# Post-LN linear attention and gated FFN on one NeuronCore: attention's output too is turned in 32x32 blocks and through DRAM, and the order of a pass is rewritten

## What is computed

```python
qkv = relu(einsum('bnc,oc->bno', x, qkv_weight)); q, k, v = (qkv[:, :, j] for j in range(3))   # after a reshape
v_pad = concatenate([v, ones], axis=-1)
vk = einsum('bnhe,bnhd->bhed', v_pad, k)
vk_q = einsum('bhed,bnhd->bnhe', vk, q)
att = vk_q[..., :8] / (vk_q[..., 8:] + 1e-15)
x1 = layernorm(x + einsum('bnc,oc->bno', att, proj_weight) + proj_bias)
h = silu(x1 @ (w_gate/127).T) * (x1 @ (w_up/127).T)
out = layernorm(x1 + h @ (w_down/127).T)
```

## Time and profile before

| | us |
|---|---|
| median of 3 runs | 555.39 (554.58 to 556.39) |
| the profiled execution's own time | 555.23 |
| its span in the profile | 553.3 |
| TensorE busy | 525.3 (95%) |
| VectorE busy | 409.2 (74%) |
| ScalarE busy | 223.5 (40%) |
| GpSimd busy | 89.4 (16%) |

### The profile page before, as it was taken

How to read it: one execution, slowest core, us unless ns; L and a number is a source line. 1 busy time by engine, 2 the same in 40 slices (tenths; PEclk the granted TensorE clock), 3 DMA queues, 4 the chain that set the end, 5 groups by cost and what they waited for, 6 DMA issues and landing times.

```text
span 553.3 us, 9205 instructions
## 1 busy us (share of the span) xinstructions
PE 525.3 (95%) x3419; PEld 455.5 (82%) x3419; DVE 409.2 (74%) x913; ACT 223.5 (40%) x376; POOL 89.4 (16%) x94
## 2 busy tenths in 40 slices
...
GB/s 302 155 0 78 39 99 93 115 114 63 127 38 114 114 76 152 38 102 88 114 114 71 119 39 113 114 76 152 38 106 84 114 114 71 119 3 113 39 40 39
DMA packets 27918, 51.07 MB, mean 92 GB/s; under 512 B 2304, under 2 KB 17408, under 8 KB 27904
## 3 DMA queue, kind: packets, MB, share of 16 engines
...
## 4 chain that ended last, share of the span: by engine, by line
PE 78%; DVE 11%; DMA 3%; issue 3%; ACT 2%; POOL 1%; SPq 1%; DVEq 0%; POOLq 0%; ACTq 0%
PE abcd_ps L632 27%; PE gate_ps L632 24%; PE up_ps L632 22%; PE abcd_ps L659 3%; DVE x1T_lo L377 2%; PE abcd_ps L678 2%; DVE st L440 2%; DVE r L469 2%; DMA wg_raw<-w_gate 1%; DVE h L384 1%; DMA wd_raw<-x_way 1%; DMA xT_raw<-x_chan 1%; PE abcd_ps L670 1%; ACT h_hi L269 1%; DVE h_lo L377 1%
## 5 line engine op out<-in xcount | busy, mean ns | idle before, releaser
L632 PE MATMUL gate_ps<-x1T_hi,wg_hi 128*128 128x512 f32 x192 | 78.1, 407 | 15.3 <-DVE x1T_lo L377 15.3
L274 ACT ACTIVATE silu<-gate_ps 128x512 f32<-128x512 f32 x96 | 56.9, 593 | 77.7 <-PE gate_ps L632 77.7
L226 POOL TENSOR_TENSOR ve<-mv,ln_eps 128x4 f32<-128x4 f32 (+2 forms) x36 | 12.5, 346 | 444.7 <-DVE mv L446 444.7
L269 ACT ACTIVATE h_hi<-h 128x512 fp32r<-128x512 f32 x96 | 60.2, 633 | 48.0 <-DVE h L384 48.0
L632 PE MATMUL up_ps<-x1T_lo,wu_hi 128*128 128x512 f32 x192 | 74.9, 390 | 0.0
L632 PE MATMUL gate_ps<-x1T_lo,wg_hi 128*128 128x512 f32 x192 | 74.9, 390 | 0.0
L632 PE MATMUL up_ps<-x1T_hi,wu_hi 128*128 128x512 f32 x192 | 74.9, 390 | 0.0
L384 DVE SCALAR_TENSOR_TENSOR h<-up_ps,silu 128x512 f32<-128x512 f32 x96 | 64.2, 681 | 3.8 <-ACT silu L274 3.7
L377 DVE TENSOR_TENSOR h_lo<-h,h_hi 128x512 fp32r<-128x512 f32 x96 | 62.8, 680 | 1.7
L632 PEld LDWEIGHTS gate_ps<-x1T_hi,wg_hi 128*128 128x128 f32 x192 | 36.0, 188 | 25.2 <-DVE x1T_lo L377 18.7
L266 ACT ACTIVATE kv<-abcd_ps 128x512 f32<-128x512 f32 x60 | 35.9, 600 | 46.2 <-PE abcd_ps L632 46.2
...
## 6 DMA issues: line engine op xcount, KB each, us to landing
x_raw<-x_tok SPq DMA_DIRECT2D x16, 512.0 KB, 3.8
xT_raw<-x_chan SPq DMA_DIRECT2D x15, 512.0 KB, 3.3
out<-out_sb SPq DMA_DIRECT2D x15, 512.0 KB, 2.9
x_way<-wu_raw SPq DMA_DIRECT2D x56, 128.0 KB, 2.6
wd_raw<-x_way SPq DMA_DIRECT2D x14, 512.0 KB, 3.2
x<-r SPq DMA_DIRECT2D x14, 512.0 KB, 2.9
...
```

The costliest lines, as they stand in the source:

```text
L226: nc.gpsimd.tensor_tensor(ve[:, tiles], mv[:, tiles, 1], ln_eps[:, tiles], ALU.add).then_inc(ve_ok, 1)
L269: nc.scalar.activation(dst, src, ACT.Copy).then_inc(ok, 1)
L274: nc.scalar.activation(silu[:, j % 2, :], gate_ps[j % 2][:], ACT.Silu, scale=WSCALE).then_inc(silu_ok[j], 1)
L632: last = mm(dst, lhsT, rhs, start=start and n == 0, stop=stop and n == len(pairs) - 1)
```

## The change

att of batches 2 to 15 goes the way of x1: `att_blocks` transposes it in 32x32 blocks into att_sq (memory of the raw gate weights), DMAs write it to att_way and read it back into attT_raw (memory of the raw kv weights), and `attT_hi_spread` and `attT_lo_spread` take hi and lo. Only batches 0 and 1 use `attT_of`. For x1 and att the block transposes, writes, reads and hi parts go by halves of the channels, each half with its own semaphores. The transposes now read channels s*4 + j with s running fastest; a write is one run of 2 KB per partition, and the read takes pieces of 512 B.

In the attention half TensorE does kv first, then q, vk (into bank CC), one tile of down, num, and three tiles of down. The second wait of `gate_up(b, 1)`, for the second add of r2, stands ahead of its up part. VectorE adds the epsilon (`variance`), GpSimd only takes the power. VectorE makes x1, its blocks, then h_lo of blocks 4 and 5, the output of batch i-2, vk, xT_lo two batches ahead, x1T_lo, att and its blocks of batch i+1, and only then both adds of r2 and their statistics. x and xT are loaded, and xT_hi made, a batch earlier.

The diff, cut to its core (and its margin to fit):

```diff
-x1_sq = in_place_of(wu_raw).rearrange("p (c n) -> p c n", c=NCB)
+x1_sq = in_place_of(wu_raw).rearrange("p (k n) -> p k n", k=KC)
 x1T_raw = in_place_of(wd_raw).rearrange("p (k n) -> p k n", k=KC)
-x1_way = nc.dram_tensor("x1_way", (P, KC, NG, P), FP32, kind="Internal").ap()
+att_sq = in_place_of(wg_raw).rearrange("p (k n) -> p k n", k=KC)
+attT_raw = wkv_raw[:].rearrange("p a b -> p (a b)").rearrange("p (k n) -> p k n", k=KC)
+x1_way, att_way = (nc.dram_tensor(n, (KC, P, TB), FP32, kind="Internal").ap() for n in ("x1_way", "att_way"))
...
-    def spread_x1(b):
-        sp.wait_ge(x1_sq_ok, b)
-        for g in range(NG):
-            sp.dma_start(x1_way[:, :, g, :].rearrange("(j c) k n -> c k j n", j=NG),
-                         x1_sq[g * SQ:(g + 1) * SQ].rearrange("c (k j) n -> c k j n", k=KC)).then_inc(x1_away, 16)
-        sp.wait_ge(x1_away, 16 * NG * b)
-        sp.dma_start(x1T_raw, x1_way.rearrange("p k g n -> p k (g n)")).then_inc(x1T_in, 16)
+    def write_blocks(n, sq, sq_ok, way, away):
+        for k in range(KC):
+            sp.wait_ge(sq_ok[k], n)
+            sp.dma_start(way[k], sq[:, k, :]).then_inc(away[k], 16)
+    def read_turned(n, way, away, T_raw, T_in):
+        for k in range(KC):
+            sp.wait_ge(away[k], 16 * n)
+            sp.dma_start(T_raw[:, k, :], way[k].rearrange("(g s) (j n) -> s j g n", g=NG, j=NG)
+                         .rearrange("s j g n -> (s j) g n")).then_inc(T_in[k], 16)
     def turn(i):
         any_i = not isinstance(i, int)
+        if any_i or i + 2 < NB:
+            load_xT(i + 2)
+        if any_i or 0 < i < NB - 1:
+            write_blocks(i, x1_sq, x1_sq_ok, x1_way, x1_away)
+            read_turned(i, x1_way, x1_away, x1T_raw, x1T_in)
         if any_i or i >= 2:
             sp.wait_ge(out_ok, i - 1)
             sp.dma_start(out[i - 2], out_sb[:].rearrange("p t c -> p (t c)")).then_inc(stored, 16)
-        if any_i or i + 1 < NB:
-            sp.wait_ge(xb_ok, i + 1)
-            sp.dma_start(x_raw[:], x[i + 1]).then_inc(x_in, 16)
         if any_i or i + 2 < NB:
-            load_xT(i + 2)
+            sp.wait_ge(xb_ok, i + 2)
+            sp.dma_start(x_raw[:], x[i + 2]).then_inc(x_in, 16)
         if any_i or 0 < i < NB - 1:
-            spread_x1(i)
+            write_blocks(i, att_sq, att_sq_ok, att_way, att_away)
             sp.wait_ge(r2_ok[1], i)
             sp.dma_start(x1[:], r1[:]).then_inc(x1_copied, 16)
+            read_turned(i, att_way, att_away, attT_raw, attT_in)
     sp.dma_start(xT_raw[:, 0, :], xT[0][:, 0, :]).then_inc(xT_half_in[0], 16)
...
-    def rstd(b, mv, mv_ok, ve, ve_ok, rs, rs_ok, tiles=slice(0, NT)):
-        pool.wait_ge(mv_ok, b + 1)
-        nc.gpsimd.tensor_tensor(ve[:, tiles], mv[:, tiles, 1], ln_eps[:, tiles], ALU.add).then_inc(ve_ok, 1)
+    def rstd(b, ve, ve_ok, rs, rs_ok, tiles=slice(0, NT)):
         pool.wait_ge(ve_ok, b + 1)
         nc.gpsimd.tensor_tensor(rs[:, tiles], ve[:, tiles], minus_half[:, tiles], ALU.pow).then_inc(rs_ok, 1)
...
-    with pool.Fori(1, NB - 1) as i:
-        pool.wait_ge(den_ok, i + 1)
+    xb_of(1)
+    rstd_1(1)
+    with pool.Fori(2, NB - 1) as i:
+        pool.wait_ge(h_lo_ok[NH - 1], i - 1)
         xb_of(i)
+        rstd_2(i - 2)
         rstd_1(i)
-        rstd_2(i - 1)
-    pool.wait_ge(den_ok, NB)
+    pool.wait_ge(h_lo_ok[NH - 1], NB - 2)
     xb_of(NB - 1)
+    rstd_2(NB - 3)
...
+    def attT_hi_spread(b):
+        act.wait_ge(proj_mm[1], b)
+        for k in range(KC):
+            act.wait_ge(attT_in[k], 16 * (b - 1))
+            rounded(by_token(attT_hi, k), spread(attT_raw, k), attT_hi_ok[k])
     def x1T_hi_spread(b):
         act.wait_ge(up_mm[NH - 1], b)
-        act.wait_ge(x1T_in, 16 * b)
-        for k in range(KC):
-            rounded(by_token(x1T_hi, k), x1T_spread(k), x1T_hi_ok[k])
+        for k in range(KC):
+            act.wait_ge(x1T_in[k], 16 * b)
+            rounded(by_token(x1T_hi, k), spread(x1T_raw, k), x1T_hi_ok[k])
...
+    def step(i):
+        for j in range(NH - 2):
+            silu_of(i - 1, j)
+            if j < NH - 3:
+                h_hi_of(i - 1, j)
+        if isinstance(i, int) and i == 1:
+            attT_hi_of(i)
+        else:
+            attT_hi_spread(i)
+        h_hi_of(i - 1, NH - 3)
+        silu_of(i - 1, 4)
+        silu_of(i - 1, 5)
         h_hi_of(i - 1, 4, 5)
-        if qkv:
+        if not isinstance(i, int) or i < NB - 1:
+            for t in range(NT):
+                kv_relu(t, i + 1, abcd[:, t, :])
             q_relu(i + 1)
-            for t, bank in enumerate((CC, D, A, B)):
-                kv_relu(t, i + 1, bank)
+            if not isinstance(i, int) or i + 2 < NB:
+                xT_hi_of(i + 2)
             x1T_hi_spread(i)
...
+    def variance(b, mv, mv_ok, ve, ve_ok, tiles=slice(0, NT)):
+        dve.wait_ge(mv_ok, b + 1)
+        nc.vector.tensor_scalar(ve[:, tiles], mv[:, tiles, 1], LN_EPS, None, ALU.add).then_inc(ve_ok, 1)
...
+    def blocks_turned(sq, r, oks):
+        for k in range(KC):
+            nc.vector.transpose(sq[:, k, :].rearrange("p (j t s) -> p t j s", j=NG, t=NT),
+                                r[:, :, k * P:(k + 1) * P].rearrange("p t (s j) -> p t j s", j=NG)).then_inc(oks[k], 1)
     def x1_blocks(b):
         dve.wait_ge(x1_ok, b + 1)
-        nc.vector.transpose(x1_sq.rearrange("p c (t s) -> p t c s", t=NT),
-                            r1[:].rearrange("p t (c s) -> p t c s", s=SQ)).then_inc(x1_sq_ok, 1)
+        blocks_turned(x1_sq, r1, x1_sq_ok)
+    def att_blocks(b):
+        dve.wait_ge(att_ok, b + 1)
+        blocks_turned(att_sq, att, att_sq_ok)
+    def T_lo_spread(b, T_raw, T_hi, T_hi_ok, T_lo, T_lo_ok):
+        for k in range(KC):
+            dve.wait_ge(T_hi_ok[k], b + 1)
+            minus_hi(by_token(T_lo, k), spread(T_raw, k), by_token(T_hi, k)).then_inc(T_lo_ok[k], 1)
+    def attT_lo_spread(b):
...
     def ffn_half(i):
-        att_of(i)
+        late = not isinstance(i, int) or i > 1
+        if late:
+            dve.wait_ge(st2_ok, i - 1)
         h_of(i - 1, 0)
-        if not isinstance(i, int) or i > 1:
-            out_of(i - 2)
+        if late:
+            aggregated(st2, mv2, mv2_ok)
+            variance(i - 2, mv2, mv2_ok, ve2, ve2_ok)
         h_of(i - 1, 1)
-        h_lo_of(i - 1, 0, 1)
+        h_lo_of(i - 1, 0)
         h_of(i - 1, 2)
-        if not isinstance(i, int) or i < NB - 1:
-            xT_lo_of(i + 1)
+        h_lo_of(i - 1, 1)
         h_of(i - 1, 3)
-        attT_lo_of(i)
-        h_lo_of(i - 1, 2, 3)
-        h_of(i - 1, 4, 5)
+        if late:
+            attT_lo_spread(i)
+        else:
+            attT_lo_of(i)
+        h_lo_of(i - 1, 2)
+        h_of(i - 1, 4)
+        h_lo_of(i - 1, 3)
+        h_of(i - 1, 5)
...
-        h_lo_of(i - 1, 4, 5)
+        variance(i, mv1, mv1_ok, ve1, ve1_ok)
         x1_of(i, r1)
         x1_blocks(i)
-        r2_add(i - 1, 0, x1)
-        dve.wait_ge(r2_ok[0], i)
+        h_lo_of(i - 1, 4, 5)
+        if not isinstance(i, int) or i > 1:
+            out_of(i - 2)
+        vk_of(i + 1)
+        if not isinstance(i, int) or i + 2 < NB:
+            xT_lo_of(i + 2)
+        x1T_lo_spread(i)
+        att_of(i + 1)
+        att_blocks(i + 1)
+        for n in range(2):
+            r2_add(i - 1, n, x1)
+        dve.wait_ge(r2_ok[1], i)
         stats(st2, r2, 0)
-        vk_of(i + 1)
-        r2_add(i - 1, 1, x1)
-        dve.wait_ge(r2_ok[1], i)
         stats(st2, r2, 1, st2_ok)
...
     i = NB - 1
     ffn_half(i)
     h_lo_of(i - 1, 4, 5)
+    out_of(i - 2)
     r1_of(i, pairs=True)
...
-            if j == 1 and (not isinstance(b, int) or b > 0):
+            late = j == 1 and (not isinstance(b, int) or b > 0)
+            if late:
                 pe.wait_ge(r2_ok[0], b)
-                pe.wait_ge(r2_ok[1], b)
...
+            if late:
+                pe.wait_ge(r2_ok[1], b)
             add_up(up, up_hi[:-1], stop=False)
...
         pe.wait_ge(xT_lo_ok, i + 2)
+        for t in range(NT):
+            if t >= 2:
+                pe.wait_ge(r1_ok[t - 2], i + 1)
+            kv_of(t, i + 1, abcd[:, t, :])
+        for k in range(KC):
+            pe.wait_ge(kv_ok[k], i + 2)
         q_of(i + 1)
-        for t, bank in enumerate((CC, D, A, B)):
-            if t < 2:
-                pe.wait_ge(r1_ok[t], i + 1)
-            else:
-                pe.wait_ge(q_ok[t - 2], i + 2)
-            kv_of(t, i + 1, bank)
-        down_of(i - 1, (0, 1))
         vk_of(i + 1)
-        down_of(i - 1, (2, 3))
+        down_of(i - 1, (0,))
         num_of(i + 1)
+        down_of(i - 1, range(1, NT))
```

More of the change, by code:

```diff
@@ L24 @@
 SQ = 32
-NG, NCB = P // SQ, C // SQ
+NG = P // SQ
 BANK = 512
@@ L132, in build @@
         x1T_mm, x1T_hi_ok, x1T_lo_ok = signals("x1T_mm", KC), signals("x1T_hi_ok", KC), signals("x1T_lo_ok", KC)
-        x1_copied, x1_sq_ok, x1_away, x1T_in = signal("x1_copied"), signal("x1_sq_ok"), signal("x1_away"), signal("x1T_in")
+        x1_copied = signal("x1_copied")
```

(21 more changed lines are left out.)

59 lines of the change are left out of this document (26 added, 33 removed).

## The result

The changed kernel takes 557.98 us (median of 20 runs, 554.93 to 560.54), the kernel before 554.86 us (20 runs, 553.02 to 556.62). The ratio is 1.0044, with a 95% interval of 1.0027 to 1.0062: **slower by 0.4%**, where 533.4 us was forecast and a range of 528.5 to 548. The profiled execution took 555.09 us for a span of 552.9, 0.4 less than the span before.

What follows compares the result with a forecast made beforehand. TensorE (31.4 us a pass) and a ring through VectorE (31.3) were taken as level bounds; 31.5 a pass saves 1.67 in 14 passes, 23.4, less 1.5 at the ends: 533.4 us from 555.3, range 528.5 to 548.

Steps and rivals of the forecast that it cites:

- TensorE's sum: TensorE's work in one loop pass without att's transposes and the x1T_lo stall: 31.38 us, 1.79 less per pass.
- The ring: Loop's chain of work and waits from r1's first add to the next pass's: 31.3 us, level with TensorE's 31.4.
- the price of the strided transposes: VectorE's block transposes reading every fourth channel, 16 bytes apart: no extra cost taken, bounds nothing and a doubling.
- the walk: Step-by-step sum of the ring's times from r1's first add: 31.7 us, less 0.4 for overlaps, 31.3.
- moves under the output's normalisation: GpSimd's x+bias (2.4 us) shifts beside VectorE's output step in the loop, said to cost nothing.
- the rule that the prediction itself quoted: Skill's SBUF rule: each access crossing to a new 16-byte line pays a penalty of unstated size; every new transpose element does.
- The trip through DRAM: Write and read back of one 256 KB half: 5.8 us, bounds 4.3 and 7.7, VectorE's near 5 us beside it.
- SP's worst place: att's reads queued behind the copy of r1: done at 27.0 at worst, wanted at 27.5 to 28, so covered.
- Numerators ahead of three tiles of down: TensorE's order, one down tile covering vk: hidden if TensorE is slower, costs up to 0.6 where the ring is.
- The ends: First and last batches outside the steady loop: 1.5 us lost in all, 1.1 of it in the last batch.
- the ring is longer: Rival, 19%: slow transfer, slowed silu chain or late att reads make passes of 32.0 to 32.9, 540 to 552 us.
- strided transposes: Rival, 12%: transposes at double price, 2.4 us a pass on the ring, 33.7 a pass, 564 us; slower from 1.8.

Runs made afterwards that it cites:

- e3: Changed kernel with the edits of e1 and e2 together; output not the reference's: 529.45 us, ratio 0.955 to the kernel before.
- e2: Changed kernel with block transposes reading neighbouring channels, not every fourth; output not the reference's: 538.25 us, ratio 0.971 to the kernel before.
- e1: Changed kernel with GpSimd's x+bias started behind den of the same half, not behind h_lo: 547.07 us, ratio 0.988 to the kernel before.
- e5: Changed kernel with VectorE taking vk ahead of the output's normalisation: 550.13 us, ratio 0.994 to the kernel before.
- e4: Changed kernel with ScalarE taking the silu of block j+1 ahead of h_hi of block j: 548.99 us, ratio 0.991 to the kernel before.
- e6: Changed kernel with the 8 transposes of att put back on TensorE, results unused: 561.22 us, ratio 1.0126 to the kernel before.

## Why the prediction was wrong

**TensorE's sum was right but for 0.45 us.** 31.38 a pass was forecast; 30.93 is what e3 has, without a wait. That is 6 us in 14 passes, and one reason why e3 ends below the forecast. The difference is in restarts and modelled ends: three tiles of down and one 5.93 for 6.05, numerators 1.87 for 2.05, gate, up and proj 13.78 for 14.01.

**The ring was the right bound, its length was not.** I walked it to 31.3 and put it level with TensorE; it is 33.14. Two terms failed, both taken at nothing: the price of the strided transposes, worth 1.4 us a pass (33.13 to 31.74 in e2; from e1 to e3 32.33 to 30.93), and that of GpSimd's x+bias, worth 0.8 (33.13 to 32.33 in e1; from e2 to e3 31.74 to 30.93). Since TensorE sets the pass in e3, each is worth at least that. With only one of them the time stays inside the stated range of 528.5 to 548: 547.07 us in e1, just inside, and 538.25 in e2. Against the walk's points, counted from the first add of r1:

| point | walk | measured |
|---|---|---|
| x1 done | 6.4 | 6.0 |
| its transposes done | 7.75 | 8.1 |
| x1T_lo done | 14.8 | 15.8 |
| att done | 17.5 | 18.5 |
| its transposes, r2, statistics done | 21.8 | 23.3 |
| first h done | 22.5 | 24.0 |
| fourth h done | 28.1 | 29.6 |
| next r1 | 31.3 | 33.1 |

- *One failed step, the smaller in the time*, is the one sentence on GpSimd: its x+bias "moves under the output's normalisation", at no cost. It is 2.14 us, on one instruction that stands still. I took 1.4 to 1.7 for an output of 3.52. The trace of before shows it, and I did not ask. The three rows below are its timeline of GpSimd, that of VectorE, and the tile's own view (ns).

```profile
243.55 2.40 POOL L240 TENSOR_TENSOR xb<-x_raw,bias_sb 128x1024 f32<-128x1024 f32 x1
```

```profile
245.35 1.73 DVE L474 TENSOR_SCALAR out_sb<-r,mv,rstd 128x256 f32<-128x256 f32 x4
```

```profile
L474 DVE TENSOR_SCALAR out_sb<-r,mv,rstd x12: 401/402/756, 212.2 to 279.8; 128x256 f32<-128x256 f32 x12
```

  What I had charged as "up to 0.3" was the end of an overlap that the change then made whole. The Trainium skill (SBUF — State Buffer, section "Who interferes with whom") says that the one contention between engines is a port pair that VectorE and GpSimd share, held by one of them for a whole instruction while the other fully blocks, and that not every instruction of VectorE uses it. The runs agree in both: the output's instruction took 2.55 us against 0.40 to 0.41, and the reciprocal, att and vk, of which att and vk read PSUM, went on unchanged beside the same x+bias (e1, e5).
- *The other failed step, the larger one: the price of the strided transposes* was taken as nothing, against the rule that the prediction itself quoted. The truth lies between my two ends: 0.38 to 0.41 a half where a doubling was 0.6, so 1.6 us of the 2.4. By the rival's own threshold, 1.8 us on the ring, it would not have decided alone; e1, which has it alone, is indeed faster than before. That "nothing in any row" spoke for or against it was no reason for 12%, since the one rule that bore on it was for it.
- *The trip through DRAM* was sized nearly right. I took 5.8 us from the transposes; it was 5.05 in the changed kernel and 5.6 in e1, where it shows: there the second half is in x1T_lo's hands 6.3 us behind the end of its transpose (265.82 - 257.49 - 2.06), and some 0.65 of that is ScalarE's x1T_hi. In the changed kernel it hid: VectorE had 6.35 us of work between the transposes and x1T_lo (268.03 - 261.68), no more than the 6.4 that the walk gives to the trip and x1T_hi. That is the main reason why 2.14 and 1.6 us of excess lengthened the ring by 1.8 and not by 3.7. Another is luck: the walk was 0.4 too long up to x1, and 0.4 again in the adds and statistics of r2 (3.04 for 2.61).
- *The copy of r1 and att's reads* ("SP's worst place") held: attT_lo waits for nothing in the loop of the changed kernel. In e4, where the chain ahead of it is shorter, it waits for ScalarE's place in its order and still not for the read.
- *Numerators ahead of three tiles of down.* "Costs up to 0.6 where the ring is" had the right place. With the ring at 33.13 it is the whole gap, 1.72. e5 shows that the order is not its cause.
- *The ends.* Last batch: 1.3 us lost for x_last (1.9 us of waiting against 0.6), where 1.1 was forecast. Not seen: the first x1, 3.40 us instead of 1.4, again beside x+bias.

The sum then is: 0.04 us a pass, 0.6 in 14, less 1.3 more of waiting for x_last and 1.5 for the first x1, 2.2 us slower. Runs at nearly full clock say about the same. With a clock of 0.997 or more the changed kernel took 554.9 to 555.8 us (5 runs), the kernel before 552.1 to 555.4 with a median of 552.9 (24 runs, those beside the experiments, on other chips). The rivals had both mechanisms in some form ("the ring is longer", "strided transposes"), but each alone; I never added them up on the one ring on which both lie.

What stays open: why runs of the changed kernel are granted a lower clock more often. It was 0.992 or less in 13 of its 20 runs, and in 6 of the 42 of the kernel before beside the experiments. In the profiles with such a stretch most of it lies in the prologue (e6: 0.66 between 40 and 50 us). No run isolates the reason.
